# Seven of each chunk's 21 down products move from fp32 to three rounded passes, with GpSimd subtracting the remainders

## The reference

```python
x = x + 0.5 * ffn(layernorm(x))
x = x + attn(layernorm(x))       # a = layernorm(x); a + softmax attention(a), 16 heads of 64, causal
x = x + 0.5 * ffn(layernorm(x))

# ffn of one row h (128 numbers)
scores = sigmoid(h @ gate_weight.T)                  # 32 experts in 4 groups
top-2 groups by scores + gate_bias, then top-6 experts; weights scaled to sum 0.2
routed = sum_e cw[e] * ((silu(h @ w_gate[e]) * (h @ w_up[e])) @ w_down[e])     # 64 wide each
shared = (silu(h @ shared_w_gate) * (h @ shared_w_up)) @ shared_w_down         # 64 wide
anchor = the same form, one of 16 small experts (32 wide), picked by the first expert
out = routed + shared + 0.1 * anchor
```

## Time and profile before

| | |
|---|---|
| three runs, median | 1450.74 us |
| the profiled execution, device time | 1452.6 us |
| its span | 1450.8 us |
| granted TensorE clock, mean | 0.995 |
| PE busy | 1412.9 us (97%) |
| DVE busy | 1111.2 us (77%) |
| ACT busy | 800.2 us (55%) |
| POOL busy | 287.6 us (20%) |

### The profile page before, as it was taken

One profiled execution on the slowest core, in us unless ns is written; L12 is line 12 of the kernel. 1 busy time (PEld: TensorE's weight loads), 2 busy tenths in 40 slices (PEclk: granted clock), 3 DMA queues, 4 the chain that ended last, 5 costly groups with the idle time before them and its releaser, 6 DMA issues.

```text
span 1450.8 us, 27512 instructions
## 1 busy us (share of the span) xinstructions
PE 1412.9 (97%) x9680; PEld 967.3 (67%) x9680; DVE 1111.2 (77%) x2521; ACT 800.2 (55%) x1909; POOL 287.6 (20%) x586
## 2 busy tenths in 40 slices
PE   5999999999989999999999999999899999999998
PEld 4666666666657667676766676676566666666665
DVE  8888888887677777777777777778767877787775
ACT  4344344433457777777777877777544233423422
POOL 1000000000124434444443444344400000000000
PEclk9999999999999999999999999999999999999999
DMA  6432323332300000000000000000033333333332
GB/s 231 162 132 105 112 97 124 107 117 97 116 30 2 2 2 2 2 2 1 2 2 2 2 2 2 1 2 2 2 120 104 126 109 121 110 119 116 119 112 87
DMA packets 59025, 98.07 MB, mean 68 GB/s; under 512 B 6160, under 2 KB 15504, under 8 KB 58896
## 3 DMA queue, kind: packets, MB, share of 16 engines
q1 hardware_dynamic: 58896, 96.38, 19.6%
HBM read 92.68 MB, written 3.67 MB: 66 GB/s over the span
## 4 chain that ended last, share of the span: by engine, by line
PE 86%; DVE 8%; ACT 3%; issue 2%; POOL 0%; DMA 0%; SPq 0%; POOLq 0%; DVEq 0%; ACTq 0%
PE banks L424 19%; PE banks L199 14%; PE banks L201 13%; PE banks L200 13%; PE banks L560 10%; PE banks L525 7%; PE banks L546 5%; PE banks L383 2%; PE banks L535 2%; DVE nmax L1297 2%; ACT work L859 1%; PE banks L395 1%; DVE q_lo L1286 1%; DVE ctx_lo L1317 1%; DVE stage L1312 1%
## 5 line engine op out<-in xcount | busy, mean ns | idle before, releaser
L803 ACT ACTIVATE work<-banks 128x512 f32<-128x512 f32 x320 | 190.9, 597 | 444.5 <-PE banks L201 435.2
L424 PE MATMUL banks<-work,wd 128*128 128x512 f32 x672 | 342.8, 593 | 0.6 <-DVE work L1179 0.4
L1205 DVE TENSOR_TENSOR work<-banks,work 128x512 f32<-128x512 f32 x320 | 220.7, 690 | 147.8 <-ACT work L803 143.4
L859 ACT ACTIVATE work<-banks,nmax 128x512 f32<-128x512 f32 (+3 forms) x512 | 264.4, 528 | 51.9 <-DVE nmax L1297 47.7
L1454 POOL TENSOR_SCALAR work<-work,rrec 128x512 f32<-128x512 f32 (+3 forms) x512 | 261.7, 533 | 0.0
L199 PE MATMUL banks<-xT_hi,wg_hi 128*128 128x512 f32 x336 | 248.0, 738 | 0.5 <-DVE wu_lo L1170 0.4
L1179 DVE TENSOR_TENSOR work<-work 128x512 f32<-128x512 f32 x320 | 226.7, 709 | 5.6 <-DMA work<-cw_rows 1.5
L1297 DVE TENSOR_REDUCE nmax<-banks 128x2 f32<-128x1024 f32 (+3 forms) x256 | 195.6, 806 | 3.1 <-PE banks L535 3.1
L1312 DVE COPY stage<-banks 128x1024 f32<-128x1024 f32 (+1 forms) x128 | 121.9, 952 | 57.9 <-PE banks L546 57.7
L424 PEld LDWEIGHTS banks<-work,wd 128*128 128x128 f32 x672 | 126.2, 189 | 35.3 <-DVE work L1179 4.1
L201 PE MATMUL banks<-xT_hi,wg_lo 128*128 128x512 f32 x336 | 133.4, 397 | 0.0
(11 more groups left out here) (140 smaller groups left out, 2189.6 us busy)
## 6 DMA issues: line engine op xcount, KB each, us to landing
work<-cw_rows SPq DMA_DIRECT2D x320, 256.0 KB, 3.0
x<-in_x SPq DMA_DIRECT2D x8, 256.0 KB, 6.4
out_rows<-x SPq DMA_DIRECT2D x8, 256.0 KB, 2.2
cw_rows<-cwT SPq DMA_DIRECT2D x16, 96.0 KB, 1.9
stage<-in_w_gate SPq DMA_DIRECT2D x3, 448.0 KB, 4.9
wd<-in_w_down SPq DMA_DIRECT2D x3, 448.0 KB, 7.6
stage<-in_w_up SPq DMA_DIRECT2D x2, 448.0 KB, 6.4
stage<-in_wq SPq DMA_DIRECT2D x1, 512.0 KB, 3.8
```

The source lines that it names most:

```text
L424: pe.matmul(psY, wd[:, j * P:(j + 1) * P], z[part_slot(j)], start=j == 0, stop=j == HT - 1, skip_group_check=True).then_inc(s["down_ps"], 1)
L803: nc.scalar.activation(silu[j % 2], psG[j % 3], ACT.Silu) \
L859: m = nc.scalar.activation(prob[:, p % 2, i, o:o + w], ps[:, i, so:so + w], ACT.Exp, bias=nmax[:, p % 2, i, qb:qb + 1], accum_out=rsum[:, ...
L1205: tt(gated[j % 3], psU[j % 3], silu[j % 2], ALU.mult) \
```

## The change

Tiles 0 to 4, 18 and 19 of every chunk (`SPLIT_Z`) have their down product as three rounded passes. In the first chunk tiles 0 to 4 stay in fp32. For each such tile ACT copies z into the rounded type (`z_high`), POOL subtracts that copy from z (`z_low`), and PE waits for POOL's semaphore instead of DVE's. The parts lie in the attention's q and k tiles, a ring of four. The weights of the seven tiles are stored first, are loaded into the staging buffer and split once, by ACT in slot 10 of the first chunk and by POOL. Parts of the old buffers shrink to make room (`cw` has 48 columns in place of 128, `wts` shares `masked`, and `sc` and `chosen` lie in the stage), so one memset goes. Two small steps of the first stage move: the statistics of the chunk after next from slots 3 and 4 to 6 and 9, and their square root on ACT from slot 8 to 12. SP waits for the split down weights and for the first five down products before it loads the attention's weights into the stage.

```diff
+SPLIT_Z = [0, 1, 2, 3, 4, 18, 19]
+DOWN_ORDER = SPLIT_Z + [j for j in range(HT) if j not in SPLIT_Z]
-        wd = sb("wd", [P, HC])
+        wd = sb("wd", [P, HC - GT * P])
+        wd_parts = [sb(f"wd_{n}", [P, GT * P], F32R) for n in ("hi", "lo")]
+        z_parts = [[t[:, i, :] for t in qk[n] for i in (0, 1)] for n in (0, 1)]
+        def splits(g, j):
+            return g * len(SPLIT_Z) - 5 + SPLIT_Z.index(j) + 1
+        def split_z(g, j):
+            return j in SPLIT_Z and not (g == 0 and j < 5)
...
+            sp.wait_ge(wd_split, 1)
+            sp.wait_ge(s["down_ps"], 5)
...
             def down(g, j, first):
-                pe.wait_ge(s["z_done"], tiles(g, j))
...
+                if split_z(g, j):
+                    pe.wait_ge(s["z_lo"], splits(g, j))
+                    if g == 0:
+                        pe.wait_ge(wd_split, 1)
+                    mm3(pe, psY, [w[:, c] for w in wd_parts], [t[splits(g, j) % 4] for t in z_parts],
+                        j == 0, False).then_inc(s["down_ps"], 1)
+                    return
+                pe.wait_ge(s["z_done"], tiles(g, j))
...
+            def z_high(g, j):
+                act.wait_ge(s["z_done"], tiles(g, j))
+                nc.scalar.activation(z_parts[0][splits(g, j) % 4], z[part_slot(j)], ACT.Copy) \
+                    .then_inc(s["z_hi"], 1)
...
-                    if 0 < g < NC - 2 and j == 8:
+                    if 0 < g < NC - 2 and j == 12:
                         row_std(g + 2)
...
                     if j == 2 and not first:
                         y_copy(g - 1)
+                    if setup and j == 10:
+                        act.wait_ge(wd_loads[0], 16)
+                        nc.scalar.activation(wd_parts[0][:, :], stage[:, 0, 2, :], ACT.Copy) \
+                            .then_inc(wd_split_hi, 1)
+                    if setup and j == 20:
+                        z_high(0, 18)
+                    elif not setup and split_z(g, j - 1):
+                        z_high(g, j - 1)
+                if setup:
+                    z_high(0, 19)
...
-                at_input_stats = 18 if setup else 3
+                at_input_stats, at_input_mean = (18, 19) if setup else (6, 9)
...
+            pool.wait_ge(wd_split_hi, 1)
+            nc.gpsimd.tensor_tensor(wd_parts[1][:, :], stage[:, 0, 2, :], f32(wd_parts[0][:, :]),
+                                    ALU.subtract).then_inc(wd_split, 1)
+            def z_low(g, j):
+                pool.wait_ge(s["z_hi"], splits(g, j))
+                nc.gpsimd.tensor_tensor(z_parts[1][splits(g, j) % 4], z[part_slot(j)],
+                                        f32(z_parts[0][splits(g, j) % 4]), ALU.subtract) \
+                    .then_inc(s["z_lo"], 1)
+            for g in range(NC - 1):
+                for j in SPLIT_Z:
+                    if split_z(g, j):
+                        z_low(g, j)
+            for j in SPLIT_Z[:5]:
+                z_low(NC - 1, j)
             ...
+            for j in SPLIT_Z[5:]:
+                z_low(NC - 1, j)
...
+            for g in range(NC, 2 * NC):
+                for j in SPLIT_Z:
+                    z_low(g, j)
```

More of the change, by code:

```diff
@@ L134, in build @@
         score = sb("score", [P, TB, E])
-        sc = sb("sc", [P, TB, E])
+        sc, chosen = [stage_flat[:, 4 * PW + i * TB * E:4 * PW + (i + 1) * TB * E]
+                      .rearrange("p (t e) -> p t e", t=TB) for i in (0, 1)]
         t4 = [sb(f"t4_{i}", [P, TB * G, 4]) for i in range(2)]
@@ L147, in build @@
         onehot = sb("onehot", [P, TB, E, TOPK])
-        chosen = sb("chosen", [P, TB, E])
-        wts = sb("wts", [P, TB, E])
+        wts = masked
         wsum = sb("wsum", [P, TB, 1])
@@ L153, in build @@
         anch = sb("anch", [P, TB, L])
-        cw = sb("cw", [P, TB, P])
+        cw = sb("cw", [P, TB, ROWS])
         cwT = sb("cwT", [ROWS, CH])
         qk = [[sb(f"{m}_{n}", [P, 2, CH], F32R) for n in ("hi", "lo")] for m in "qk"]
+        z_parts = [[t[:, i, :] for t in qk[n] for i in (0, 1)] for n in (0, 1)]
         ctx_parts = [sb(f"ctx_{n}", [P, CH], F32R) for n in ("hi", "lo")]
@@ L187, in build @@
         spread_loads = [sem(f"s_spread{k}") for k in range(NSPREAD)]
+        wd_split_hi, wd_split = sem("s_wd_split_hi"), sem("s_wd_split")
         wsplit_hi = [sem(f"s_wsplit_hi{k}") for k in range(W_GROUPS)]
@@ L228, in part_slot_free, with down_columns @@
             return tiles(g, j) - (HT if j == HT - 1 else 4 if j > 3 else 5)
+        def splits(g, j):
+            return g * len(SPLIT_Z) - 5 + SPLIT_Z.index(j) + 1
+        def split_z(g, j):
+            return j in SPLIT_Z and not (g == 0 and j < 5)
+        def down_columns(j):
+            o = DOWN_ORDER.index(j) % GT if j in SPLIT_Z else DOWN_ORDER.index(j) - GT
+            return slice(o * P, (o + 1) * P)
         ROUTE = 37
@@ L305, in load_down @@
                 cols = slice(k * GT * P, (k + 1) * GT * P)
-                sp.dma_start(wd[:, cols], wd_in[:, cols]).then_inc(wd_loads[k], 16)
+                dst = stage[:, 0, 2, :] if k == 0 else wd[:, (k - 1) * GT * P:k * GT * P]
+                sp.dma_start(dst, wd_in[:, cols]).then_inc(wd_loads[k], 16)
             def load_x(sp, c):
@@ L403, in prep_cwT @@
                 pe.wait_ge(s["route"], (g + 1) * ROUTE)
-                to_columns(ps, cw).then_inc(s["cwT_ps"], 1)
+                to_columns(ps[0:ROWS, :], cw).then_inc(s["cwT_ps"], 1)
             def gate_up(g, j, first):
@@ L418, in down @@
             def down(g, j, first):
-                pe.wait_ge(s["z_done"], tiles(g, j))
+                c = down_columns(j)
                 if j == 0 and not first:
                     pe.wait_ge(s["y_evac"], g)
-                if first and g == 0 and j % GT == 0:
-                    pe.wait_ge(wd_loads[j // GT], 16)
-                pe.matmul(psY, wd[:, j * P:(j + 1) * P], z[part_slot(j)], start=j == 0,
+                if split_z(g, j):
[6 more added lines that the diff above has]
+                pe.wait_ge(s["z_done"], tiles(g, j))
+                if first and g == 0:
+                    pe.wait_ge(wd_loads[DOWN_ORDER.index(j) // GT], 16)
+                pe.matmul(psY, (stage[:, 0, 2, c] if j in SPLIT_Z else wd[:, c]), z[part_slot(j)], start=j == 0,
                           stop=j == HT - 1, skip_group_check=True).then_inc(s["down_ps"], 1)
@@ L1227, in ffn_chunk @@
                         rows_stats(g + 2)
-                    if g < NC - 2 and j == at_input_stats + 1:
+                    if g < NC - 2 and j == at_input_mean:
                         rows_mean(g + 2, input_stats(g + 2))
@@ L1405, in attention @@
                 dve.wait_ge(s["out_added"], NC)
-            nc.vector.memset(cw[:, :, ROWS:], 0.0)
             nc.vector.memset(z[part_slot(HT - 1)][0:MI, :], 0.0)
@@ L1493 @@
         "w_up": hidden_columns(L0_ffn_w_up, L0_ffn_anchor_w_up, []),
-        "w_down": down.reshape(HT, P, D).transpose(1, 0, 2).reshape(P, HT * D),
+        "w_down": down.reshape(HT, P, D)[DOWN_ORDER].transpose(1, 0, 2).reshape(P, HT * D),
         "gate_weight": np.asarray(L0_ffn_gate_weight).T,
```

## The result

The changed kernel takes 1448.49 us, median of 17 runs (1445.1 to 1450.6), against 1450.56 for the kernel before, also 17 runs: ratio 0.9985, 95% interval [0.9979, 0.9992]. One run of the kernel before, at 1747.21 us, is in its median but not in the ratio. The gain is 2.1 us where 10.2 were forecast. The direction was right and the time lies in the range, but the size was wrong by 8 us, and a gain of this size is one that the forecast had called not to be told from none (under 2.9 us), though the interval leaves out 1.

The account below looks back on a forecast made before the run. PE, busy 97% of the span, was taken as the bound: 18.4 us saved less 2.8 and 0.7 at joints and 4.7 at three places gives 10.2, so 1440.5 us from 1450.74; range 1435.5 to 1450.5.

Parts of the forecast that it names:

- What bounds it: Whole kernel: PE, busy 97% of the span; time taken from PE comes off until DVE is late.
- The price of a product: Down products: fp32 costs 0.868 us, three rounded passes 0.696; 0.172 us less each, 18.4 us for 107.
- rival 5: Down products: three passes adding to the same bank don't get cheaper; about 1450 us, chance 0.04.
- Copy and subtraction: Each split tile, 512 columns: ACT's copy takes 0.62 us, POOL's subtraction 1.25 us.
- rivals 3 and 4: POOL first each time, serial chain: 2.53 us a tile, 1447.6 us, chance 0.14; dearer subtraction 2.69 us, 1456.0 us, chance 0.10.
- The joints of the first stage: Where chunks meet: z(0) late, PE waits 0.4 us at the first down product, 2.8 us in 7 joints.
- rival 2: Chunk joints: normalise's one-input operations also wait for POOL's subtraction; 2.8 us in 7 first-stage joints, 1443.3 us, chance 0.12.
- The joints of 0 and 1, and of 8 and 9: Counted as ordinary joints, at 0.4 us in the first stage and 0.1 us in the second.
- The very end: Last products wait for the copy and subtraction: 1.3 us, or 2.1 if POOL's subtraction comes first.
- Start of the second stage and end of the first: Places without a slot of cover: waits cost 1.6 us at the start, 1.5 us at the end.
- The moved statistics: First stage, slots 3 and 4 to later slots: room for DVE where split tiles are, load carried to slot 18.
- The test that I had set: Prediction wrong if PE idles over 0.9 us at a first-stage joint, or the three uncovered places cost over 6 us.

Follow-up runs that it names:

- x6: Changed kernel with each of the 107 split products as one fp32 product, copy and subtraction still waited for: 1461.68 us, ratio 1.0074.
- x1: Changed kernel without GpSimd's subtractions of z, PE waiting for ScalarE's copy instead: 1438.67 us, ratio 0.9920.
- x3: Changed kernel with seven of the 107 split products, at the ends, back in fp32: 1442.38 us, ratio 0.9942.
- x10: Changed kernel with ScalarE's square root ahead of the copies of tiles 18 and 19 at joints 0 to 1 and 8 to 9: 1448.90 us, ratio 0.9989.
- x8: Changed kernel with 16 products back in fp32, 91 in three passes, GpSimd's subtractions in place: 1439.22 us, ratio 0.9922.
- x5: Changed kernel with only the program's last two split products back in fp32: 1444.96 us, ratio 0.9959.
- x9: Kernel before with only the moved statistics and square root, all down products in fp32: 1450.10 us, ratio 0.9996.
- x2: Changed kernel with PE's transposes of the next chunk's normalised rows one slot later: 1448.69 us, ratio 0.9987.

## Why the prediction was wrong

- **What bounds it** was right: PE. Periods follow PE's passes wherever PE doesn't wait, and DVE at 48 of 55 us does not set the pace by itself (x6).
- **The price of a product** was a little high. Rounded down passes stand 0.23 us apart as forecast (1435.81 to 1436.04 above), which settles rival 5, but seven products gave 1.12 us and not 1.20: 0.160 for 0.172, in sum 1.3 us. The 0.868 came from one slot of rows rounded to 0.01 us, and an error of 0.01 in it is 1 us in 107 products; the period of a chunk is the better ruler.
- **Copy and subtraction** were right: 0.62 to 0.63 us, and 1.26 to 1.30 us by itself for 1.25. Its median is 1.29, and its mean of 1.46 us holds waits for VectorE, up to 1.76. The z product's median is 0.69 us as before, so it comes first mostly, and rivals 3 and 4, the serial chain, did not come about.
- **The joints of the first stage** had the right size (0.47 for 0.4) for the wrong reason. The step had z(0) late and PE waiting at the first down product. In fact VectorE's one-input operations wait for the subtraction too, the normalise comes late, and PE waits at the transposes. This is rival 2's mechanism: a copy of 128x4 took 0.82 to 0.84 us for 0.17 at these joints, and the 64x512 operation (L1226) had a median of 1528 ns over its 16 instances for 424, most of them in the second stage. In x1, without the subtractions, no instance of either was over 0.22 and 0.43 us. The sign that the prediction had named for it, normalise rows over 0.5 us, did not come: they stayed at 0.34. The Trainium skill's rule in "SBUF — State Buffer", section "SBUF: two separate sides", that VectorE's two-port modes take the exclusive lock as well as its two-input operations, agrees with these rows; which mode an instruction ran in the trace doesn't show. I had given the rival 0.12 though no row spoke against it. In an ordinary joint its 0.4 stood in place of the forecast's 0.4 and not on top of it, so its time of 1443.3 would not have come out either.
- **The joints of 0 and 1, and of 8 and 9**, were the step that failed most (3.2 of the 8 us): they were counted as two of fourteen equal joints at 0.4 and 0.1 us and cost 2.2 and 1.5. I had cost ScalarE's copies as hidden because it is busy 22.7 of 55 us. At these two joints the copies come in front of a square root with its table load, on which the normalise depends, and they wait there for z. The order of instructions on ScalarE showed that ahead of time; I did not go through what stood behind each added copy. x3 and x10 tell apart how much: at 8 to 9 the order is 0.4 us and VectorE's waits behind GpSimd most of the rest; at 0 to 1 the root, the wait of tile 18 and the late copy of yT take one another's place, and taking all of them away (x8) brings the joint to 48.48.
- **The very end** failed by 2.1 us. 0.7 of it is the order that I had named and not taken (the z product behind the subtraction, 1434.31, 1.66 us; 2.1 us for 1.3), 1.4 the clock, for which the sum had no term: it counted the last products at the upper level. x5 shows the whole: 3.5 us back for two products.
- **Start of the second stage and end of the first** were right: 1.8 for 1.6, 1.3 for 1.5.
- **The moved statistics** at nothing: right (x9).
- **The test that I had set** (wrong if the three places cost over 6 us) came out at 6.8, and so did the second (over 0.9 us of idle time at a joint), at 0 to 1. Both pointed to the right place.

The other entries of the table are small: 0.4 us more in the steady joints of either stage, 0.2 at the start.

What stays open is when the clock falls. It fell behind 1.58 and 1.59 us of waiting at the very end in all three profiles that have it, and behind 1.86 in x1; it did not behind 1.42 in x6, 1.52 at the start of the second stage, 1.30 at the joint of 8 and 9, or 1.90 at the joint of 0 and 1 in x10. And one wait can go either way: at the end of the first stage PE waited 2.42 to 2.44 us for GpSimd in the changed kernel, x2, x5, x6 and x10, and the clock fell in x2, x5 and x6 alone. The scatter of the runs goes with it: the two runs of the changed kernel with a mean granted clock of 0.998 took 1445.1 and 1446.7 us, the nine with 0.994 took 1448.5 to 1450.6. How much of it is the end and how much the attention stage isn't settled.

## What to carry to other kernels

Cheaper instructions behind a longer chain pay inside a steady stretch and lose where chunks meet and stages end: price each of those places by itself, with what stands behind every added instruction on its own engine's queue, a table load above all. Then use the new form only where the chain has time; here 91 of the 107 products give about five times the gain of all of them (11.6 us and 2.1). If moving a waiting instruction a slot later changes nothing (x2), the late engine is the cause: take work off it at that spot (x8), not the waiter out of its way.

## What the runs showed of the hardware that I had not expected

- A VectorE operation with one input, from SBUF to SBUF, waits for a running GpSimd subtraction as a two-input one does: 64x512 in 1.53 us (median) for 0.42, and a copy of 128x4 in 0.84 for 0.17.
- The granted clock can fall within the last 10 us of a kernel behind one wait, with passes 0.43 us apart for 0.23; that cost 1.4 us, and it came in each of the three profiles with that wait. Behind a wait of 1.86 us in x1 it did so for six passes in the middle of the work. But the same wait of 2.4 us at the end of the first stage had a fall with it in three of five profiles.
- A ScalarE copy ran straight behind a square root (1102.20, then 1102.34) with no table load between; the load came only before the next Silu.
- The attention stage, the same code, took 631.60 to 634.05 us in these profiles, by where the granted clock fell (at 437 us and before the second stage in the slowest; in x8's profile at the first place alone): profiles can differ by more than this change is worth without a change in the code.
